# A fused gather, gated FFN and residual on one NeuronCore: the per-tile quantisation of the hidden layer rebuilt

## The chip, the cores and the metric

One NeuronCore of a Trainium2 chip runs the whole program. The metric is the device time of one execution in microseconds (us); lower is better. The engines are PE (TensorE), DVE (VectorE), ACT (ScalarE), POOL (GpSimd) and SP (SyncE, which here only starts DMAs). Each works through its own instruction stream in order, and streams meet only at semaphores.

## The reference

The input is 1024 rows (32 batches of 32 channels) by 256 features. Cut to what matters:

```python
w  = cond_weights[itok]                                   # one 32x32 matrix per batch
xc = einsum('bct,bcd->bdt', x, w)                         # small mix of channels
def act_quant(x):                                         # row-wise, 8 bits
    scale = 127.0 / clip(max|x|, 1e-4)
    return clip(round(x * scale), -128, 127) / scale
def linear_bit(x, w, g):                                  # w ternary: round(tanh(w/mean|w|)) * arctanh(mean|w|)
    return einsum('bsd,od->bso', act_quant(g * x * rsqrt(mean(x*x) + 1e-8)), ternary(w))
h   = silu(linear_bit(xc, w1, g1)) * linear_bit(xc, w2, g2)   # 256 -> 1024
out = x + linear_bit(h, w3, g3)                               # 1024 -> 256
```

The part of interest is the last line's quantisation of h: for each row, the mean of the squares of 1024 hidden values, the largest |h * g3|, the rounding of h * g3 to integers of at most 127, and a factor that puts the scale back after the last matmul.

## The kernel before

Rows are cut into 8 tiles of 128 (TILES). A head loads and ternarises the three weight matrices, gathers the small matrices, mixes the channels and quantises x; it lasts until about 34 us. Then a pipeline over the tiles runs. Its stages for tile t, each a closure of that name on one engine:

- PE `up_a(t)`, `up_v(t)`: four 128x512 matmuls each into a_ps and v_ps. Both accumulators exist once, so `up_a(t+1)` waits for `silu(t)` and `up_v(t+1)` for `hidden(t)`.
- ACT `silu(t)` (L399) reads a_ps and writes gate. DVE `hidden(t)` (L551) multiplies v_ps, its scale and gate into hid.
- POOL L325 writes hg = hid * g3 for the whole 1024 columns. ACT `squares(t)` (L406) sums hid squared into h_ss and throws the squares away.
- POOL `h_roots(t)`: two [128,1] steps (L309, L311) and a power (L316) on two columns give the root of the mean square and its inverse.
- DVE `peak_of(t)` (L560) is an absolute maximum over hg, `step_of` (L566) and `scale_of` (L574) turn it into the step and its reciprocal.
- ACT `rounding(t)` (L413) writes hr = hg * scale + a large constant, in fp32; the integer, plus 1536, then stands as an fp16 number in the low half of each word.
- PE `h_turn(t)` (L758) transposes these halves into t_ps, DVE `keep_h(t)` (L581) subtracts 1536 and writes bf16, PE `down(t)` (L769) multiplies with the third weight, POOL `h_deq_of(t)` (L302) forms the output factor, DVE `residual(t)` (L588) adds the result to x_sb, and SP stores the tile.

Buffers of hid, hg, hr and of the statistics are two deep. The order on each engine is written out by hand. POOL does, for t = 0 to 6: L325 of t, `h_roots(t)`, `h_deq_of(t-1)`. For the last tile POOL does no L325: DVE does that product itself (`gain_last`, L596) and also the rounding (`rounding_last`, L602). At the end PE runs `h_turn(7)`, `down(6)`, `down(7)`.

Two operations of the head matter below: POOL's `round_w` (L237, one operation over 2048 columns) and DVE's `diagonal` (L446, four small copies from SBUF to SBUF).

Of the kernel before, what the change touches and what calls it, by code (L numbers as in the profile page):

```python
# [6 lines left out]
FP16 = mybir.dt.float16  # L7
INT32 = mybir.dt.int32
# [5 lines left out]
P = 128  # L14
# [14 lines left out]

OFFSET = 1536.0  # L30
# [3 lines left out]
def adaln_ffn(nc, x, cond, cond_w, w1, g1, w2, g2, w3, g3, out):  # L34
    ctx = ExitStack()
    with ctx:
# [44 lines left out]
        h_sq_junk = sb("h_sq_junk", [P, 2, HID], BF16)  # L81
# [13 lines left out]
        hid = sb("hid", [P, 2, HID])  # L95
        hg = sb("hg", [P, 2, HID])
        hr = sb("hr", [P, 2, HID])
        hq_t = sb("hq_t", [P, 2, KH, P], BF16)
        h_ss = sb("h_ss", [P, 2])
        h_base = sb("h_base", [P, 2, 2])  # L100
        h_root = sb("h_root", [P, 2, 2])
        h_peak = sb("h_peak", [P, 2])
        h_step = sb("h_step", [P, 2])
        h_scale = sb("h_scale", [P, 2])
        h_deq0 = sb("h_deq0", [P, 2])
# [34 lines left out]
        xr_last, hr_last = sem("xr_last"), sem("hr_last")  # L140
        hg_last = sem("hg_last")
        hss_ready, hg_ready, hbase_ready, hroot_ready = sem("hss_ready"), sem("hg_ready"), sem("hbase_ready"), sem("hroot_ready")
        hpeak_ready, hstep_ready, hscale_ready, hdeq0_ready = sem("hpeak_ready"), sem("hstep_ready"), sem("hscale_ready"), sem("hdeq0_ready")
        hr_ready, ht_ready, hq_ready, y_ready, out_ready = sem("hr_ready"), sem("ht_ready"), sem("hq_ready"), sem("y_ready"), sem("out_ready")
# [49 lines left out]
        def _(pool):  # L194
# [18 lines left out]
            pool.memset(minus_one[:], -1.0).then_inc(roots_made, 1)  # L213
            pool.memset(cw_diag[:], 0.0).then_inc(diag_zero, 1)
# [66 lines left out]
            pool.wait_ge(roots_made, 3)  # L281
# [49 lines left out]
            h_deq_of(TILES - 1)

        @block.scalar
        def _(act):
# [56 lines left out]
            logarithm()  # L391
            act.wait_ge(xdeq_ready, 2)
# [22 lines left out]

            silu(0)
            for t in range(TILES):
                if t + 1 < TILES:
                    silu(t + 1)
                squares(t)  # L420
                if t >= 1:
                    rounding(t - 1)

        @block.vector
        def _(dve):
# [118 lines left out]
            def hidden(t):  # L544

                dve.wait_ge(gate_ready, t + 1)
                dve.wait_ge(v_ready, t + 1)
                if t >= 2:
                    dve.wait_ge(hss_ready, t - 1)
                    dve.wait_ge(hg_ready, t - 1)  # L550
                dve.scalar_tensor_tensor(hid[:, t % 2], v_ps[:], x_deq[:, 1, t // 2, t % 2:t % 2 + 1], gate[:, t % 2],  # L551
                                         ALU.mult, ALU.mult).then_inc(hid_ready, 1)

            def peak_of(t):
                b = slice(t % 2, t % 2 + 1)
                if t < TILES - 1:
                    dve.wait_ge(hg_ready, t + 1)
                else:
                    dve.wait_ge(hg_last, 1)
                dve.tensor_reduce(h_peak[:, b], hg[:, t % 2], AX.X, ALU.max, apply_absolute_value=True).then_inc(hpeak_ready, 1)  # L560

            def step_of(t):
                b = slice(t % 2, t % 2 + 1)
                dve.wait_ge(hpeak_ready, t + 1)
                dve.wait_ge(hroot_ready, t + 1)
                dve.tensor_scalar(h_step[:, b], h_peak[:, b], 1.0 / QMAX, h_root[:, t % 2, 0:1],  # L566
                                  ALU.mult, ALU.max).then_inc(hstep_ready, 1)

            def scale_of(t):
                b = slice(t % 2, t % 2 + 1)  # L570
                dve.wait_ge(hstep_ready, t + 1)
                if t >= 2:
                    dve.wait_ge(hr_ready, t - 1)
                dve.reciprocal(h_scale[:, b], h_step[:, b]).then_inc(hscale_ready, 1)  # L574

            def keep_h(t):

                dve.wait_ge(ht_ready, t + 1)
                if t >= 2:
                    dve.wait_ge(y_ready, t - 1)  # L580
                dve.tensor_scalar(hq_t[:, t % 2], t_ps[t % 2][:, :].rearrange("p (j n) -> p j n", j=KH), -OFFSET, None,  # L581
                                  ALU.add).then_inc(hq_ready, 1)

            def residual(t):

                dve.wait_ge(y_ready, t + 1)
                dve.wait_ge(hdeq0_ready, t + 1)
                dve.scalar_tensor_tensor(x_sb[:, t], y_ps[t % 2][:, 0:FEAT], h_deq0[:, t % 2:t % 2 + 1], x_sb[:, t],  # L588
                                         ALU.mult, ALU.add).then_inc(out_ready, 1)

            def gain_last(t):

                dve.wait_ge(hid_ready, t + 1)
                dve.wait_ge(hr_ready, t - 1)
                dve.wait_ge(g3_in, 16)
                dve.tensor_tensor(hg[:, t % 2], hid[:, t % 2], g3_all[:], ALU.mult).then_inc(hg_last, 1)  # L596

            def rounding_last(t):

                dve.wait_ge(hscale_ready, t + 1)  # L600
                dve.wait_ge(ht_ready, t - 1)
                dve.tensor_scalar(hr[:, t % 2], hg[:, t % 2], h_scale[:, t % 2:t % 2 + 1], ROUNDER,  # L602
                                  ALU.mult, ALU.add).then_inc(hr_last, 1)

            hidden(0)
            x_keep(3)
            hidden(1)
            peak_of(0)
            step_of(0)
            keep_w(2, 0)  # L610
            scale_of(0)
            keep_w(2, 1)
            for t in range(2, TILES - 1):
                hidden(t)
                peak_of(t - 1)
                if t >= 3:
                    residual(t - 3)
                step_of(t - 1)
                keep_h(t - 2)
                scale_of(t - 1)  # L620

            last = TILES - 1
            hidden(last)
            peak_of(last - 1)
            gain_last(last)
            step_of(last - 1)
            residual(last - 3)
            scale_of(last - 1)
            keep_h(last - 2)
            peak_of(last)  # L630
            step_of(last)
# [181 lines left out]
```

## Time and profile before

| | us |
|---|---|
| median of 3 runs | 77.32 |
| lowest and highest | 76.74, 77.88 |
| span of the profiled execution (first to last instruction) | 76.6 |
| busy: PE, DVE, ACT, POOL | 48.0, 58.1, 47.7, 55.4 |

The profiled execution's own time is not among those listed; the three runs lie 0.1 to 1.3 above its span. Busy sums cover head and pipeline together, so what the pipeline is limited by has to be read from the time lines of its engines. In those, each line gives start, duration, engine, source line, operation and output<-inputs; in brackets stands idle time before it and what ended it. Two consecutive operations of an engine can overlap by up to 0.1 us, so the distance of two starts is a little shorter than the duration.

### The profile page before, as it was taken

How to read it: one execution, taken by the hardware profiler on the slowest of the kernel's cores; microseconds unless marked ns; L12 is line 12 of the kernel's file. 1: busy time of each engine (PE TensorE's matmuls, PEld its weight loads, DVE VectorE, ACT ScalarE, POOL GpSimd, SP SyncE). 2: the span in 40 equal slices, each digit the busy share in tenths (PEclk: the TensorE clock that was granted, in tenths of full speed). 3: DMA queues.
4: the chain of work that ended last, by engine and by line, in shares of the span. 5: the costliest groups of instructions: out<-in, count | busy, mean ns of one | idle time of the engine just before them, and what ended most of it. 6: DMA issues, size and time to landing. Idle time of an engine off the chain costs nothing.

```text
span 76.6 us, 1068 instructions
## 1 busy us (share of the span) xinstructions
PE 48.0 (63%) x298; PEld 31.3 (41%) x302; DVE 58.1 (76%) x117; ACT 47.7 (62%) x70; POOL 55.4 (72%) x97
## 2 busy tenths in 40 slices
PE   0200509995829803999897298977888471079960
PEld 0200408774526702355461155544545250078730
DVE  0203278989999999967699989979797979996340
ACT  5014508599909995995859959896979783410000
POOL 6788777264938977989689898999999999810100
PEclk9999999999975895556999999999999999855589
DMA  0599989963710000000000000010202020010222
GB/s 0 119 385 346 327 237 278 330 210 115 253 71 0 0 0 4 0 9 4 0 0 0 0 0 4 17 52 9 68 0 68 0 68 0 23 45 0 68 68 68
DMA packets 5369, 6.22 MB, mean 81 GB/s; under 512 B 500, under 2 KB 4980, under 8 KB 5364
## 3 DMA queue, kind: packets, MB, share of 16 engines
q1 hardware_dynamic: 5108, 6.03, 24.6%
q0 software_dynamic: 256, 0.13, 0.8%
q8 instruction: 2, 0.03, 0.2%
q14 instruction: 3, 0.02, 0.1%
HBM read 5.11 MB, written 1.05 MB: 80 GB/s over the span
## 4 chain that ended last, share of the span: by engine, by line
DVE 24%; issue 22%; POOL 22%; DMA 12%; PE 11%; ACT 4%; SPq 0%; POOLq 0%; DVEq 0%
DMA w_sb<-in_L_ffn_w 12%; POOL hg L325 11%; PE y_ps L769 6%; DVE xg L477 6%; DVE cw_diag L446 5%; DVE x_peak L482 5%; PE a_ps L652 3%; PE t_ps L758 2%; POOL h_deq L302 2%; DVE hid L551 2%; ACT hr L413 2%; DVE abs_sum L438 2%; POOL h_root L316 2%; POOL h_base L311 2%; POOL h_base L309 1%
## 5 line engine op out<-in xcount | busy, mean ns | idle before, releaser
L325 POOL TENSOR_TENSOR hg<-hid,g_all 128x1024 f32<-128x1024 f32 x7 | 16.5, 2358 | 0.8 <-DVE hid L551 0.8
L413 ACT ACTIVATE hr<-hg,rounder,h_scale 128x1024 f32<-128x1024 f32 x7 | 8.7, 1241 | 5.5 <-DVE h_scale L574 5.5
L769 PE MATMUL y_ps<-w_t,hq_t 128*128 128x256 bf16 x64 | 10.3, 319 | 2.1 <-DVE hq_t L581 2.0
L560 DVE TENSOR_REDUCE h_peak<-hg 128x1 f32<-128x1024 f32 x8 | 9.7, 1217 | 1.7 <-POOL hg L325 1.6
L551 DVE SCALAR_TENSOR_TENSOR hid<-v_ps,x_deq,gate 128x1024 f32<-128x1024 f32 x8 | 10.2, 1271 | 0.9 <-PE v_ps L725 0.6
L725 PE MATMUL v_ps<-w_t,xq_t 128*128 128x512 bf16 x30 | 8.9, 415 | 3.0 <-DVE hid L551 2.9
L399 ACT ACTIVATE gate<-a_ps,x_deq 128x1024 f32<-128x1024 f32 x8 | 8.8, 1100 | 2.2 <-PE a_ps L725 2.1
L725 PE MATMUL a_ps<-w_t,xq_t 128*128 128x512 bf16 x30 | 8.7, 407 | 1.8 <-issue 1.3
L218 POOL DMA_INDIRECT cw_rows<-in_L_cond_weights,row_idx x8 | 7.9, 982 | 2.4 <-issue 2.1
L769 PEld LDWEIGHTS y_ps<-w_t,hq_t 128*128 128x128 bf16 x64 | 6.9, 115 | 5.6 <-DVE hq_t L581 4.1
L652 PE MATMUL a_ps<-x_sb,cw_diag 128*128 128x256 f32 x16 | 7.0, 597 | 2.5 <-DVE cw_diag L446 2.5
L758 PE MATMUL t_ps<-ident,hr 128*128 128x128 f16 x64 | 5.8, 243 | 4.2 <-ACT hr L413 4.2
L406 ACT ACTIVATE h_sq_junk<-hid 128x1024 bf16<-128x1024 f32 x8 | 8.4, 1046 | 0.0
L341 ACT ACTIVATE abs_values<-w_sb 128x1024 bf16<-128x1024 f32 x4 | 4.2, 1061 | 5.2 <-DMA w_sb<-in_L_ffn_w 5.2
L346 ACT ACTIVATE w_sb<-w_sb,inv_mean 128x2048 f32<-128x2048 f32 x3 | 6.0, 1999 | 2.2 <-DVE inv_mean L455 2.2
L667 PE MATMUL y_ps<-abs_sum,ones 128*128 128x1 f32 x12 | 2.5, 317 | 7.6 <-DVE abs_sum L438 7.2
L758 PEld LDWEIGHTS t_ps<-ident,hr 128*128 128x128 f16 x64 | 4.8, 110 | 6.0 <-ACT hr L413 4.7
L438 DVE TENSOR_REDUCE abs_sum<-w_sb 128x1 f32<-128x1024 f32 x2 | 2.4, 1220 | 5.4 <-DMA w_sb<-in_L_ffn_w 5.4
L302 POOL TENSOR_SCALAR h_deq<-h_step,h_root,atanh 128x1 f32<-128x1 f32 x8 | 3.6, 455 | 3.5 <-DVE x_sb L588 3.5
L316 POOL TENSOR_TENSOR h_root<-h_base,roots 128x2 f32<-128x2 f32 x8 | 5.6, 702 | 0.7
L725 PEld LDWEIGHTS v_ps<-w_t,xq_t 128*128 128x128 bf16 x32 | 2.8, 104 | 7.8 <-DVE hid L551 5.0
L581 DVE TENSOR_SCALAR hq_t<-t_ps 128x1024 bf16<-128x1024 f16 x8 | 5.5, 683 | 0.6 <-PE t_ps L758 0.6
(76 smaller groups left out, 99.9 us busy)
## 6 DMA issues: line engine op xcount, KB each, us to landing
w_sb<-in_L_ffn_w SPq DMA_DIRECT2D x6, 512.0 KB, 4.5
x_sb<-in_x SPq DMA_DIRECT2D x4, 256.0 KB, 3.1
out<-x_sb SPq DMA_DIRECT2D x8, 128.0 KB, 1.7
g_all<-in_L_ffn_g SPq DMA_DIRECT2D x1, 512.0 KB, 4.3
g<-in_L_ffn_g SPq DMA_DIRECT2D x2, 128.0 KB
cw_rows<-in_L_cond_weights,row_idx POOLq DMA_INDIRECT x8, 4.3
cond_i<-in_itok_B SPq DMA_DIRECT2D x1, 0.1 KB
```

What stands on the lines that cost most here:

```text
L218: pool.indirect_dma_start(cw_rows[:, t, :], None, cond_rows, bass.IndirectOffsetOnAxis(ap=row_idx[:, t:t + 1].bitcast(UINT32), axis=0)).th ...
L316: pool.tensor_tensor(h_root[:, b], h_base[:, b], roots[:, :, 0], ALU.pow).then_inc(hroot_ready, 1)
L325: pool.tensor_tensor(hg[:, b], hid[:, b], g3_all[:], ALU.mult).then_inc(hg_ready, 1)
L399: act.activation(gate[:, t % 2], a_ps[:], ACT.Silu, scale=x_deq[:, 0, t // 2, t % 2:t % 2 + 1]).then_inc(gate_ready, 1)
L406: act.activation(h_sq_junk[:, t % 2], hid[:, t % 2], ACT.Square, accum_out=h_ss[:, t % 2:t % 2 + 1]).then_inc(hss_ready, 1)
L413: act.activation(hr[:, t % 2], hg[:, t % 2], ACT.Identity, scale=h_scale[:, t % 2:t % 2 + 1], bias=rounder[:]).then_inc(hr_ready, 1)
L551: dve.scalar_tensor_tensor(hid[:, t % 2], v_ps[:], x_deq[:, 1, t // 2, t % 2:t % 2 + 1], gate[:, t % 2], ALU.mult, ALU.mult).then_inc(hid_ ...
L560: dve.tensor_reduce(h_peak[:, b], hg[:, t % 2], AX.X, ALU.max, apply_absolute_value=True).then_inc(hpeak_ready, 1)
L652: last = pe.matmul(xc_ps[p % 2][:, i, :], cw_diag[:, 2 * p + i, :], x_sb[:, 2 * p + i, :], start=True, stop=True)
L725: last = pe.matmul(ps[:, n * HALF:(n + 1) * HALF], xq_t[:, which, c, t * P:(t + 1) * P], w_t[which][:, c, n * HALF:(n + 1) * HALF], start= ...
L758: last = pe.transpose(t_ps[t % 2][:, j * P:(j + 1) * P], low_half(hr[:, t % 2, j * P:(j + 1) * P]), ident[:])
L769: last = pe.matmul(y_ps[t % 2][:, 0:FEAT], hq_t[:, t % 2, j, :], w_t[2][:, j, :], start=(j == 0), stop=(j == KH - 1))
```

## The change

- POOL's product with g3 covers only columns 0 to 511 (SPLIT).
- ACT's `squares` keeps its squares, in fp32, in h_sq. Once before the pipeline ACT also squares g3/127 into g3_sq. The peak is then the maximum of h_sq * g3_sq, one `tensor_tensor_reduce` on DVE.
- Step, its inverse and the root are all taken with one POOL power over three columns, after one [128,1] step (`base`) and one [128,2] step that takes the maximum with the peak.
- The rounding is the conversion to int16 on write: POOL (`rounding_p`) multiplies its half of hg, DVE (`rounding_v`) computes hid * factor * g3 for columns 512 to 1023 in one operation. No constant is added, and no 1536 has to be taken off.
- The eviction of t_ps (`keep_h`) goes from DVE to ACT, which no longer rounds; for the last tile it stays on DVE.
- POOL handles all 8 tiles alike; `gain_last` and `rounding_last` are gone. hid is three deep, the statistics four.
- PE runs `down(t-2)` after `up_v(t+1)` and `h_turn(t-1)`.

```diff
+            def gain(t):
                 pool.wait_ge(hid_ready, t + 1)
                 if t >= 2:
+                    pool.wait_ge(hr_p, t - 1)
+                pool.tensor_tensor(hg[:, t % 2], hid[:, t % DEPTH, 0:SPLIT], g3_all[:, 0:SPLIT], ALU.mult).then_inc(hg_ready, 1)
+            def base(t):
+                pool.wait_ge(hss_ready, t + 1)
...
+                pool.tensor_scalar(h_base[:, r, 2:3], h_ss[:, r:r + 1], 1.0 / HID, EPS, ALU.mult, ALU.add).then_inc(hbase_ready, 1)
+            def roots_of(t):
+                pool.wait_ge(hbase_ready, t + 1)
+                pool.wait_ge(hpeak_ready, t + 1)
+                pool.tensor_scalar(h_base[:, r, 0:2], h_base[:, r, 2:3].to_broadcast([P, 2]), FLOOR_STEP ** 2, h_peak[:, r:r + 1],
+                                   ALU.mult, ALU.max).then_inc(hstep_ready, 1)
...
+                pool.tensor_tensor(h_root[:, r], h_base[:, r], h_roots[:], ALU.pow).then_inc(hroot_ready, 1)
+            def rounding_p(t):
+                pool.wait_ge(hroot_ready, t + 1)
...
+                pool.tensor_scalar(hr[:, t % 2, 0:SPLIT], hg[:, t % 2], h_root[:, t % RING, 0:1], 1.0, ALU.mult, ALU.mult).then_inc(hr_p, 1)
+            def deq_of(t):
...
+                pool.tensor_scalar(h_deq[:, r:r + 1], h_root[:, r, 1:2], h_root[:, r, 2:3], atanh[:, 2:3],
+                                  ALU.mult, ALU.mult).then_inc(hdeq_ready, 1)
+            for t in range(TILES):
+                gain(t)
+                base(t)
+                roots_of(t)
+                rounding_p(t)
+                deq_of(t)
...
             logarithm()
+            act.wait_ge(g3_in, 16)
+            act.activation(g3_sq[:], g3_all[:], ACT.Square, scale=1.0 / QMAX).then_inc(g3sq_ready, 1)
             act.wait_ge(xdeq_ready, 2)
...
             silu(0)
             for t in range(TILES):
+                squares(t)
                 if t + 1 < TILES:
                     silu(t + 1)
-                squares(t)
                 if t >= 1:
-                    rounding(t - 1)
+                    keep_h(t - 1)
...
+            def peak_of(t):
+                dve.wait_ge(hss_ready, t + 1)
...
+                dve.tensor_tensor_reduce(hg_sq[:], h_sq[:, t % 2], g3_sq[:], 1.0, 0.0, ALU.mult, ALU.max,
+                                         h_peak[:, r:r + 1]).then_inc(hpeak_ready, 1)
+            def rounding_v(t):
+                dve.wait_ge(hroot_ready, t + 1)
...
+                dve.scalar_tensor_tensor(hr[:, t % 2, SPLIT:], hid[:, t % DEPTH, SPLIT:], h_root[:, t % RING, 0:1], g3_all[:, SPLIT:],
+                                         ALU.mult, ALU.mult).then_inc(hr_v, 1)
             hidden(0)
             x_keep(3)
+            peak_of(0)
             hidden(1)
             keep_w(2, 0)
             keep_w(2, 1)
+            rounding_v(0)
+            for t in range(1, TILES):
+                peak_of(t)
+                if t + 1 < TILES:
+                    hidden(t + 1)
+                if t >= 3:
+                    residual(t - 3)
+                rounding_v(t)
```

## Rows read from the trace of the kernel before

**Rows 1.** The page, the chain that ended last: shares of the span.
```profile
DVE 24%; issue 22%; POOL 22%; DMA 12%; PE 11%; ACT 4%; SPq 0%; POOLq 0%; DVEq 0%
```
**Rows 2.** Time line of ACT where the pipeline starts.
```profile
33.09 1.28 ACT L372 ACT_TABLE_LOAD   x1
34.47 1.11 ACT L399 ACTIVATE gate<-a_ps,x_deq 128x1024 f32<-128x1024 f32 x1
```
**Rows 3.** Time line of POOL, one turn of the pipeline; start us, us, operation.
```profile
52.76 2.35 POOL L325 TENSOR_TENSOR hg<-hid,g_all 128x1024 f32<-128x1024 f32 x1
55.19 0.19 POOL L309 TENSOR_SCALAR h_base<-h_ss 128x1 f32<-128x1 f32 x1
...
55.73 0.70 POOL L316 TENSOR_TENSOR h_root<-h_base,roots 128x2 f32<-128x2 f32 x1
56.44 0.34 POOL L302 TENSOR_SCALAR h_deq<-h_step,h_root,atanh 128x1 f32<-128x1 f32 x1
56.74 2.36 POOL L325 TENSOR_TENSOR hg<-hid,g_all 128x1024 f32<-128x1024 f32 x1
```
**Rows 4.** Busy time by stretch: PE, PEld, DVE, ACT, POOL, granted clock, DMA.
```profile
48.80:52.80 4.00, 3.53 (x27) 1.94 (x25) 3.59 (x7) 3.64 (x6) 3.75 (x7) 1.00 0.10 33
...
64.50:68.00 3.50, 0.60 (x6) 0.61 (x7) 3.46 (x7) 1.24 (x1) 2.62 (x5) 0.78 0.11 37
```
**Rows 5.** The chain that ended last, in order of time: its end.
```profile
70.14 0.85 PE t_ps L758 x8
...
73.97 0.48 DVE x_sb L588
```
**Rows 6.** Groups by line and form; columns: busy us, mean ns | idle before, releaser.
```profile
L325 POOL TENSOR_TENSOR hg<-hid,g_all 128x1024 f32<-128x1024 f32 x7 | 16.5, 2358 | 0.8 <-DVE hid L551 0.8
...
L551 DVE SCALAR_TENSOR_TENSOR hid<-v_ps,x_deq,gate 128x1024 f32<-128x1024 f32 x8 | 10.2, 1271 | 0.9 <-PE v_ps L725 0.6 <-ACT gate L399 0.3
L560 DVE TENSOR_REDUCE h_peak<-hg 128x1 f32<-128x1024 f32 x8 | 9.7, 1217 | 1.7 <-POOL hg L325 1.6
...
L399 ACT ACTIVATE gate<-a_ps,x_deq 128x1024 f32<-128x1024 f32 x8 | 8.8, 1100 | 2.2 <-PE a_ps L725 2.1
...
L406 ACT ACTIVATE h_sq_junk<-hid 128x1024 bf16<-128x1024 f32 x8 | 8.4, 1046 | 0.0
...
L588 DVE SCALAR_TENSOR_TENSOR x_sb<-y_ps,h_deq,x_sb 128x256 f32<-128x256 f32 x8 | 3.8, 478 | 2.3 <-PE y_ps L769 2.3
L237 POOL TENSOR_SCALAR w_sb<-w_sb 128x2048 f32<-128x2048 f32 x2 | 3.8, 1904 | 0.0
...
L243 POOL TENSOR_SCALAR xr<-xg,x_scale 128x256 f32<-128x256 f32 x6 | 2.8, 477 | 1.6 <-DVE x_scale L493 1.5
...
L365 ACT ACTIVATE w_t<-t_ps,neg_offset 128x1024 bf16<-128x1024 f16 x2 | 2.2, 1098 | 0.0
```
**Rows 7.** Time line of POOL in the head: a long operation and two powers.
```profile
19.88 1.91 POOL L237 TENSOR_SCALAR w_sb<-w_sb 128x2048 f32<-128x2048 f32 x1
...
25.82 0.86 POOL L261 TENSOR_TENSOR lg<-lg,minus_one 128x3 f32<-128x3 f32 x1
...
32.00 0.98 POOL L269 TENSOR_TENSOR lg<-lg,minus_one 128x3 f32<-128x3 f32 x1
```
**Rows 8.** Time line of DVE in the head, the small copies.
```profile
11.69 0.90 DVE L446 COPY cw_diag<-cw_rows 32x64 f32<-32x64 f32 x4
...
20.15 2.33 DVE L446 COPY cw_diag<-cw_rows 32x64 f32<-32x64 f32 x4
```
**Rows 9.** Time line of DVE and POOL together, tiles 6 and 7.
```profile
64.26 1.22 DVE L596 TENSOR_TENSOR hg<-hid,g_all 128x1024 f32<-128x1024 f32 x1
64.43 1.26 POOL L302 TENSOR_SCALAR h_deq<-h_step,h_root,atanh 128x1 f32<-128x1 f32 x1
```
**Rows 10.** Time line of DVE at the end of the head.
```profile
32.06 1.14 DVE L502 TENSOR_SCALAR xr<-xg,x_scale 128x256 f32<-128x256 f32 x4
```

More of the change, by code:

```diff
@@ L7 @@
 FP16 = mybir.dt.float16
+INT16 = mybir.dt.int16
 INT32 = mybir.dt.int32
@@ L27 @@
 FLOOR_STEP = FLOOR / QMAX
+SPLIT = 512
+DEPTH = 3
+RING = 4
 OFFSET = 1536.0
@@ L94, in adaln_ffn @@
         gate = sb("gate", [P, 2, HID])
-        hid = sb("hid", [P, 2, HID])
-        hg = sb("hg", [P, 2, HID])
-        hr = sb("hr", [P, 2, HID])
-        hq_t = sb("hq_t", [P, 2, KH, P], BF16)
[L99 to L105, printed above, removed]
+        hid = sb("hid", [P, DEPTH, HID])
+        h_sq = sb("h_sq", [P, 2, HID])
+        g3_sq = sb("g3_sq", [P, HID])
+        hg_sq = sb("hg_sq", [P, HID], BF16)
+        hg = sb("hg", [P, 2, SPLIT])
+        hr = sb("hr", [P, 2, HID], INT16)
+        hq_t = sb("hq_t", [P, 2, KH, P], BF16)
+        h_ss = sb("h_ss", [P, RING])
+        h_peak = sb("h_peak", [P, RING])
+        h_base = sb("h_base", [P, RING, 3])
+        h_root = sb("h_root", [P, RING, 3])
+        h_roots = sb("h_roots", [P, 3])
+        h_deq = sb("h_deq", [P, RING])
         a_ps = ctx.enter_context(nc.psum_tensor("a_ps", [P, HID], FP32))
@@ L547, in hidden @@
                 dve.wait_ge(v_ready, t + 1)
[L548 to L551, printed above, removed]
+                if t >= DEPTH:
+                    dve.wait_ge(hss_ready, t - DEPTH + 1)
+                    dve.wait_ge(hg_ready, t - DEPTH + 1)
+                dve.scalar_tensor_tensor(hid[:, t % DEPTH], v_ps[:], x_deq[:, 1, t // 2, t % 2:t % 2 + 1], gate[:, t % 2],
@@ L578, in keep_h, with keep_h_last @@
+            def keep_h_last(t):
                 dve.wait_ge(ht_ready, t + 1)
[L579 to L582, printed above, removed]
+                dve.wait_ge(y_ready, t - 1)
+                dve.tensor_copy(hq_t[:, t % 2], t_ps[t % 2][:, :].bitcast(INT16).rearrange("p (j n) -> p j n", j=KH)).then_inc(hq_last, 1)
@@ L584, in residual @@
             def residual(t):
+                r = t % RING
                 dve.wait_ge(y_ready, t + 1)
-                dve.wait_ge(hdeq0_ready, t + 1)
-                dve.scalar_tensor_tensor(x_sb[:, t], y_ps[t % 2][:, 0:FEAT], h_deq0[:, t % 2:t % 2 + 1], x_sb[:, t],
+                dve.wait_ge(hdeq_ready, t + 1)
+                dve.scalar_tensor_tensor(x_sb[:, t], y_ps[t % 2][:, 0:FEAT], h_deq[:, r:r + 1], x_sb[:, t],
                                          ALU.mult, ALU.add).then_inc(out_ready, 1)
[L591 to L596, printed above, removed]
@@ L629, in _ @@
-            keep_h(last - 2)
-            peak_of(last)
-            step_of(last)
-            scale_of(last)
-            rounding_last(last)
-            keep_h(last - 1)
-            residual(last - 2)
-            keep_h(last)
-            residual(last - 1)
-            residual(last)
+                rounding_v(t)
+            residual(TILES - 3)
+            keep_h_last(TILES - 1)
+            residual(TILES - 2)
+            residual(TILES - 1)
         @block.tensor
@@ L757, in h_turn @@
                 for j in range(KH):
-                    last = pe.transpose(t_ps[t % 2][:, j * P:(j + 1) * P], low_half(hr[:, t % 2, j * P:(j + 1) * P]), ident[:])
+                    last = pe.transpose(t_ps[t % 2][:, j * P:(j + 1) * P], hr[:, t % 2, j * P:(j + 1) * P].bitcast(FP16), ident[:])
                 last.then_inc(ht_ready, 1)
             def down(t):
-                pe.wait_ge(hq_ready, t + 1)
+                if t < TILES - 1:
+                    pe.wait_ge(hq_ready, t + 1)
+                else:
+                    pe.wait_ge(hq_last, 1)
                 if t >= 2:
@@ L778, in _ @@
                     up_a(t + 1)
-                if t >= 3:
-                    down(t - 3)
-                if t + 1 < TILES:
                     up_v(t + 1)
@@ L785, in _ @@
                     w_turn(2, 1)
+                if t >= 1:
+                    h_turn(t - 1)
                 if t >= 2:
-                    h_turn(t - 2)
-            h_turn(TILES - 2)
-            down(TILES - 3)
+                    down(t - 2)
             h_turn(TILES - 1)
```

129 lines of the change are left out of this document (42 added, 87 removed).

## The prediction

> **What bounds the kernel now.** I read the chain of waits first: no engine has more than a quarter of it [rows 1], so the stages have to be taken apart. The head ends when ACT starts the first `silu` at 34.47 [rows 2]. Behind it the time line of POOL is closed: between two starts of L325 lie 56.74 - 52.76 = 3.98 us, filled without a gap by the product (2.36), two small steps, the power (0.70) and `h_deq` (0.34) [rows 3]. The other engines have slack in such a turn: of 4.00 us PE is busy 3.53, DVE 3.59, ACT 3.64, and POOL's 3.75 are its durations without the gaps of 0.08 between dependent steps [rows 4]. So POOL sets the pace of the pipeline, about 4.0 us per tile. The drain is the last transposes, two `down` and the last residual [rows 5].
>
> **POOL's own work per tile.** Removed: half of the product. Between 2358 ns for 1024 columns and about 190 ns for one of one column, half the columns cost 190 + 1084 = 1.27 us [rows 3, 6]. Two small steps (0.27 from start to start each) stay two. The power has three columns instead of two: 0.86 and 0.98 for a 128x3 power [rows 7] against 0.70; I take 0.98. Added is `rounding_p`, 512 columns from one tensor: from 477 ns at 256 and 1904 at 2048 columns [rows 6], 0.797 ns a column, 0.68 us. That it writes int16 is shown by no row; bounds: 0.68 and, at the rate of the two-input product, 1.27. I take 0.68, since reading one tensor is what it shares with those rows. `deq` stays (0.34, 0.30 to the next start). From start to start: 1.35 + 0.27 + 0.27 + 1.05 + 0.68 + 0.30 = 3.92. POOL, the bound, is thus not relieved: 3.98 becomes 3.92.
>
> **The other engines.** DVE loses the reduction (1.22), step, reciprocal (0.4) and eviction (0.68), and gains the multiply-and-max and `rounding_v`. The former is on no row; the nearest are the 1024-column operations of 1217 and 1271 ns [rows 6], the upper bound is two passes, 2.4. I take 1.22. `rounding_v`: 1271 at 1024 and 478 at 256 columns give 1.035 ns a column, 0.74 us for 512. Its turn is 1.22 + 1.27 + 0.48 + 0.74 = 3.7, less overlaps 3.4. ACT: 1.10 + 1.24 + 1.10 = 3.4; the fp32 squares are costed as the bf16 ones, the eviction at L365's 1.10 with 1.0 as the other end [rows 6]. PE does the same work. All of this is under POOL's turn and costs nothing there; if POOL's turn were under 3.4 they would be next. The deeper rings only take away waits, and none of these is in POOL's closed turn. The two added memsets and their wait stand before the gathers on POOL; DVE's first copy out of the gathered rows starts at 11.69 without having waited for them [rows 8]. I take nothing; some 0.3 us is the most, if that cover were gone.
>
> **What the change adds to the path: the port that DVE and POOL share.** Two places of the trace show the two engines excluding each other. At 64.43 POOL's `h_deq` of one column takes 1.26 instead of 0.34; everything it waits for by semaphore is past by then, but DVE's L596, a product of two tensors in SBUF, runs 64.26 to 65.48, and `h_deq` ends at 65.69, 0.21 behind it [rows 3, 9]. The other way round, DVE's four copies take 2.33 instead of 0.90, while POOL's L237 runs 19.88 to 21.79 [rows 7, 8]. And the pipeline of before avoids the clash: its `hidden` has one SBUF tensor (v_ps is in PSUM), its reduction one, its evictions none, and L325 takes 2.36 beside them each time. The changed DVE operations do not: the multiply-and-max reads h_sq and g3_sq, `rounding_v` reads hid and g3_all, all in SBUF, in each tile. A power is an exception: L269 (32.00, 0.98) runs beside DVE's four L502, which take 1.14 for all four, so neither waited for the other's end [rows 7, 10], 0.12 above the other power at most.
>
> Now the circle of dependences from power(t) to power(t+1). On POOL: `rounding_p`, `deq`, `gain`, `base`, step, power. On DVE behind power(t): `rounding_v(t)`, then `peak_of(t+1)`, for which POOL's step of t+1 waits. `hidden` and `residual` (no clash) fall under the power. The two clashing DVE operations thus lie where POOL has only reading work to do. Waiting hides the start of the blocked operation, so a blocked one costs its columns: by DVE's 0.96 to 1.03 ns a column 0.56 for `rounding_v`, 1.10 for the peak; of POOL's small one behind DVE 0.21 [rows 9]. Sum: 0.07 + 0.66 `rounding_p` + 0.56 + 0.21 `deq` + 0.05 + 1.25 `gain` + 1.10 peak + 0.15 `base` + 0.27 step + 0.98 power = 5.30; with the peak before `gain`, where nothing hides `gain`'s start, 5.48. I take 5.4 per tile.
>
> That DVE's two-input operation also waits while POOL is reading is not on these rows: the copy in [rows 8] is of another kind. If only POOL waits, the peak overlaps what POOL has begun: 5.1. I take 5.4, both ways, since each engine has been seen waiting for the other once. The Trainium skill, page "SBUF — State Buffer", section "Who interferes with whom", has it go both ways: a DVE instruction with two SBUF inputs contends with a GpSimd instruction that reads SBUF, and whichever starts first keeps the pair for the whole instruction. By that rule the turn is the 5.4, without it 5.1; the trace agrees with the half of it that has POOL waiting (1.26 for 0.34).
>
> **The start.** ACT's square of g3 (1.05 by L406 [rows 6]) comes behind the table load, which ends at 34.37, and in front of `silu(0)`, which nothing else holds back by more than 0.1 [rows 2]: `silu(0)` moves to 35.4. Nothing is there to cover it, 0.95. `hidden(0)` follows 0.1 behind its end, 36.6 to 37.85, `squares(0)`, now first in ACT's queue, to 39.1, `gain(0)` to 39.25, the peak 39.25 to 40.4, `base`, step and power to 42.0. (`silu(1)`, queued behind `squares(0)`, ends at 40.2, in time for `hidden(1)` at 40.4.) Without the clash power(0) ends at 41.75.
>
> **The end.** Power(7) ends at 42.0 + 7 x 5.4 = 79.8. Both halves of the rounding, one after the other: 0.07 + 0.66 + 0.56, hr is there at 81.1, PE starts at 81.2. From `h_turn(7)` on the order is the old one, and from its start at 70.14 to the end of the span were 6.46 us [rows 5]: 87.7. PE had fallen to a lower clock there (0.78 in the stretch before [rows 4]) after waiting, and will have waited again. The span is 76.6 and the median 77.32, so 0.7 is added: 88.4, rounded to **88.5**, 14% above before.
>
> **Rivals.**
> A, the likeliest, is this: exclusion, 5.1 to 5.5 per tile. With the first operation not waiting, 7 x 0.3 less: 86.3; with `rounding_p` at 1.27, 4.7 more: 93.1.
> B, no exclusion for these forms, against which the one case of [rows 9] speaks (it is a single one, and behind a [128,1] operation; no row has a long POOL operation against DVE's two-tensor read): POOL's 3.92 is the turn; 41.75 + 27.4 + 0.1 + 0.74 + 0.1 + 6.46 = 76.6, plus 0.7: 77.3, no change. It is the case on the other side, and decides if the two clashing operations together cost under 0.2 per tile (8 x 0.2 = 1.6, 2%). Below 75.8 it would have to be that also power and gain are at their lower ends, 0.86 and half of 2.36 (0.2 a tile, 1.6 in all): 75.7.
> C, the exclusion is shared by columns, not by whole instructions, so that half of the 1.5 us remains: 4.65 per tile; 42.0 + 32.6 + 1.4 + 6.46 + 0.7 = 83.1. The 1.26 of [rows 9] speaks against it, since a one-column operation would have slipped in.
> D, multiply-and-max takes two passes, 2.4: 1.1 a tile more than A, 97. Nothing in the trace speaks for it; no row of such an operation exists.
> E, the clock falls inside the pipeline, since PE then works 3.5 of 5.4 instead of 3.5 of 4.0. At the lower level PE's own work would be near the turn; it stayed at 1.00 in all full turns before [rows 4]. It would add one to three us to A.
>
> **How the numbers follow.** A 0.70, E (with A) 0.05, C 0.08, B 0.10, D 0.07. Slower by over 2%: all of A, E, C and D less the 0.01 that the upper end of C's sharing could leave unmeasurable: 0.89. Within 2%: B but for 0.03, and that 0.01: 0.08. Faster: the lower ends of B, 0.03. (2% is about what a measurement of this kernel tells from no change.) The range is that of A with its bounds and of C at its low end: 82.5 to 93.5. It leaves out B and D and the edge of C, 2 in 10.
>
> **What would show it.** Right: `gain` and `rounding_p` on POOL with some instances far above 1.27 and 0.68, or the small POOL steps at over 1 us, just when DVE's multiply-and-max or `rounding_v` runs; a POOL turn of 5.1 to 5.5; the first `silu` about 0.95 later, behind the square of g3. Wrong: turns near 3.9 with POOL's durations at their bare values (B), DVE's peak at 2.4 (D), granted clock under 1.00 in the middle (E). The forecast falls if the clashing operations find POOL idle or in its power more often than the circle above allows.

## The result and the profile after

The changed kernel takes 90.51 us (median of 4 runs, 88.83 to 91.15) against 77.6 for the one before. Some executions of most kernels here are in a slower state, and leaving those out (two of the four of the changed kernel, the profiled one among them) it takes 1.157 times as long, 95% interval 1.137 to 1.178. By the medians it is slower by 12.9 us, inside the predicted range of 82.5 to 93.5 and 2.0 above the 88.5.

| us | before | after |
|---|---|---|
| span of the profiled execution | 76.6 | 89.4 |
| busy PE, DVE, ACT, POOL | 48.0, 58.1, 47.7, 55.4 | 51.0, 55.9, 47.5, 68.3 |
| POOL's turn in the pipeline | 3.98 | 5.57 |

The profiled execution of the changed kernel is its longest one, 91.15; the other three have spans of 88.4, 87.1 and 89.1. DVE and ACT have less to do than before, PE the same operations, and POOL, which gave up half of the product and got half of the rounding, should have the same work by the prediction's count (3.92 for 3.98 a tile); yet it is busy for 13 us more. That contradiction is the case. In what follows a turn is the distance between two starts of the same operation in consecutive tiles, and a bare duration is the one that an operation has when nothing holds it. The first place to look is the time line of POOL, one turn (start us, us, operation; it answers [rows 3]):

```profile
53.10 2.30 POOL L337 TENSOR_SCALAR hr<-hg,h_root 128x512 int16<-128x512 f32 x1
55.38 0.34 POOL L344 TENSOR_SCALAR h_deq<-h_root,atanh 128x1 f32<-128x1 f32 x1
55.68 1.27 POOL L308 TENSOR_TENSOR hg<-hid,g_all 128x512 f32<-128x512 f32 x1
57.03 0.19 POOL L316 TENSOR_SCALAR h_base<-h_ss 128x1 f32<-128x1 f32 x1
57.33 0.29 POOL L323 TENSOR_SCALAR h_base<-h_base,h_peak 128x2 f32<-128x2 f32 x1
57.70 0.87 POOL L329 TENSOR_TENSOR h_root<-h_base,h_roots 128x3 f32<-128x3 f32 x1
58.67 2.30 POOL L337 TENSOR_SCALAR hr<-hg,h_root 128x512 int16<-128x512 f32 x1
```

From start to start: 2.28 + 0.30 + 1.35 + 0.30 + 0.37 + 0.97 = 5.57, and the six full turns from 47.52 to 80.98 are all 5.57 or 5.58. Every operation has its expected length (the power 0.87 where 0.98 was taken) but `rounding_p` (L337), 2.30 for work of 0.69. Its bare length is in this trace too: for tile 0 it takes 0.70, at 42.04, while DVE evicts w_t from PSUM. Now DVE in the same stretch:

```profile
53.03 0.75 DVE L596 SCALAR_TENSOR_TENSOR hr<-hid,h_root,g_all 128x512 int16<-128x512 f32 x1 [2.49 <-POOL h_root L329]
53.70 1.22 DVE L588 CUSTOM_DVE_ANT_0 hg_sq<-h_sq,g_sq 128x1024 bf16<-128x1024 f32 x1
54.84 0.08 DVE L588 DVE_READ_ACCUMULATOR2_ANT h_peak<- 128x1 f32 x1
54.89 1.28 DVE L578 SCALAR_TENSOR_TENSOR hid<-v_ps,x_deq,gate 128x1024 f32<-128x1024 f32 x1
```

`rounding_v` and the multiply-and-max (the custom operation L588, with its accumulator read) run 53.03 to 54.92, and `rounding_p`, started 0.07 later, ends 0.48 behind them. It is the picture of [rows 9], now in the six tiles 1 to 6 and behind two DVE operations in a row. A third view, the groups by line (busy us, mean ns | idle before), shows what waits for what elsewhere:

```profile
L337 POOL TENSOR_SCALAR hr<-hg,h_root 128x512 int16<-128x512 f32 x8 | 15.7, 1966 | 0.8
L596 DVE SCALAR_TENSOR_TENSOR hr<-hid,h_root,g_all 128x512 int16<-128x512 f32 x8 | 6.0, 750 | 15.6 <-POOL h_root L329 15.6
...
L440 ACT ACTIVATE hq_t<-t_ps 128x1024 bf16<-128x1024 int16 x7 | 7.2, 1024 | 14.6 <-PE t_ps L748 14.6
```

DVE stands 15.6 us in front of `rounding_v` until POOL's power is done, ACT 14.6 in front of the eviction: POOL's closed turn is what all others wait for. POOL never stands idle in these turns, so its busy share reads as work what is in part waiting inside an operation.

Between the two profiled executions 12.8 us divide like this. Power(0) ends at 41.94, before at 40.82 (+1.1). From there to the end of power(7) pass 38.94, before 26.19 (+12.75; of this 7 x 1.59 = 11.1 are the turn of 5.57 against 3.98, the rest mostly that the last turn used to be 2.59, the last tile's product being done by DVE). From power(7) to the end pass 8.5, before 9.6 (-1.1).

### The profile page after: what moved, and what is told of

It reads as the page before. It is cut to its first block, busy times and chain, and to the rows that moved or that the text cites. A ratio compares the mean times of both kernels' runs of the same rounds, so it can differ in the third digit from the quotient of the medians.

```text
span 89.4 us, 1071 instructions
## 1 busy us (share of the span) xinstructions
PE 51.0 (57%) x298; PEld 31.9 (36%) x302; DVE 55.9 (62%) x108; ACT 47.5 (53%) x71; POOL 68.3 (76%) x108
## 3 DMA queue, kind: packets, MB, share of 16 engines
HBM read 5.11 MB, written 1.05 MB: 69 GB/s over the span
## 4 chain that ended last, share of the span: by engine, by line
POOL 32%; DVE 22%; PE 13%; issue 11%; DMA 10%; ACT 7%; POOLq 2%; SPq 0%; DVEq 0%
DMA w_sb<-in_L_ffn_w 10%; POOL hg L308 10%; POOL hr L337 8%; POOL h_root L329 7%; PE y_ps L762 6%; DVE xg L504 5%; DVE cw_diag L473 4%; DVE x_peak L509 4%; POOL h_deq L344 3%; POOL h_base L316 2%; PE a_ps L644 2%; POOL h_base L323 2%; PE t_ps L748 2%; DVE hg_sq L588 2%; POOLq L40 1%
## 5 line engine op out<-in xcount | busy, mean ns | idle before, releaser
L337 POOL TENSOR_SCALAR hr<-hg,h_root 128x512 int16<-128x512 f32 x8 | 15.7, 1966 | 0.8
L596 DVE SCALAR_TENSOR_TENSOR hr<-hid,h_root,g_all 128x512 int16<-128x512 f32 x8 | 6.0, 750 | 15.6 <-POOL h_root L329 15.6
L440 ACT ACTIVATE hq_t<-t_ps 128x1024 bf16<-128x1024 int16 x7 | 7.2, 1024 | 14.6 <-PE t_ps L748 14.6
L308 POOL TENSOR_TENSOR hg<-hid,g_all 128x512 f32<-128x512 f32 x8 | 11.1, 1387 | 1.7 <-DVE hid L578 1.7
L762 PE MATMUL y_ps<-w_t,hq_t 128*128 128x256 bf16 x64 | 12.2, 360 | 0.0
L717 PE MATMUL a_ps<-w_t,xq_t 128*128 128x512 bf16 x28 | 10.2, 481 | 3.5 <-ACT gate L423 1.9
L578 DVE SCALAR_TENSOR_TENSOR hid<-v_ps,x_deq,gate 128x1024 f32<-128x1024 f32 x8 | 10.2, 1281 | 1.7 <-ACT gate L423 1.7
L717 PE MATMUL v_ps<-w_t,xq_t 128*128 128x512 bf16 x32 | 10.1, 447 | 0.8 <-DVE hid L578 0.8
L432 ACT ACTIVATE h_sq<-hid 128x1024 f32<-128x1024 f32 x8 | 8.4, 1051 | 3.6 <-DVE hid L578 3.6
L588 DVE CUSTOM_DVE_ANT_0 hg_sq<-h_sq,g_sq 128x1024 bf16<-128x1024 f32 x8 | 9.8, 1226 | 0.6 <-ACT h_sq L432 0.6
L329 POOL TENSOR_TENSOR h_root<-h_base,h_roots 128x3 f32<-128x3 f32 x8 | 7.0, 870 | 0.7
```

Source lines behind the costliest of these rows:

```text
L308: pool.tensor_tensor(hg[:, t % 2], hid[:, t % DEPTH, 0:SPLIT], g3_all[:, 0:SPLIT], ALU.mult).then_inc(hg_ready, 1)
L329: pool.tensor_tensor(h_root[:, r], h_base[:, r], h_roots[:], ALU.pow).then_inc(hroot_ready, 1)
L337: pool.tensor_scalar(hr[:, t % 2, 0:SPLIT], hg[:, t % 2], h_root[:, t % RING, 0:1], 1.0, ALU.mult, ALU.mult).then_inc(hr_p, 1)
L432: act.activation(h_sq[:, t % 2], hid[:, t % DEPTH], ACT.Square, accum_out=h_ss[:, t % RING:t % RING + 1]).then_inc(hss_ready, 1)
L578: dve.scalar_tensor_tensor(hid[:, t % DEPTH], v_ps[:], x_deq[:, 1, t // 2, t % 2:t % 2 + 1], gate[:, t % 2], ALU.mult, ALU.mult).then_inc( ...
L588: dve.tensor_tensor_reduce(hg_sq[:], h_sq[:, t % 2], g3_sq[:], 1.0, 0.0, ALU.mult, ALU.max, h_peak[:, r:r + 1]).then_inc(hpeak_ready, 1)
```

## Experiments

The first four runs test the suspected clash: two take one of the two clashing operations away, the third both, and the fourth puts one into the kernel before. The rival is that the wait is not at a port but in the circle of dependences. The kernels of these four compute other values than the reference, since each leaves out or changes a factor; the amount of work is what their times are about. The diffs are shortened (semaphore calls, and indices as [...]).

**The peak from one tensor.**
```diff
-dve.tensor_tensor_reduce(hg_sq[:], h_sq[:, t % 2], g3_sq[:], 1.0, 0.0, ALU.mult, ALU.max, h_peak[:, r:r + 1])
+dve.tensor_reduce(h_peak[:, r:r + 1], h_sq[:, t % 2], AX.X, ALU.max)
```


> The changed kernel with the peak as a plain maximum over h_sq (one tensor in SBUF; the factor g3 squared is left out of the peak). Same length on DVE, 1.22 us. Theory (the port of DVE's second SBUF tensor and of POOL excludes): rounding_p and what follows is no longer held for the 1.14 us of the peak, POOL's turn falls from 5.57 to about 4.4, total 90.5 - 8 x 1.14 = 81.4. Rival (the circle of dependences alone makes the turn long; rounding_p at 2.3 is merely a record that includes waiting for a semaphore): the peak still stands in the circle with the same length, 90.5.

Measured: 83.08 us (81.80 to 83.37), 1.062 times before (1.046 to 1.078), 7.4 less than the changed kernel, where 9.1 were expected. The reduction is as long as the operation it replaces, 1.21 for 1.22, and stands at the same place of the circle. It reads one tensor, and it also no longer writes a product of 1024 columns; the next run tells these two apart. In its time line, POOL and DVE together:

```profile
59.97 0.75 DVE L595 SCALAR_TENSOR_TENSOR hr<-hid,h_root,g_all 128x512 int16<-128x512 f32 x1 [1.06 <-POOL h_root L329]
60.04 1.25 POOL L337 TENSOR_SCALAR hr<-hg,h_root 128x512 int16<-128x512 f32 x1
60.64 1.21 DVE L588 TENSOR_REDUCE h_peak<-h_sq 128x1 f32<-128x1024 f32 x1
...
64.57 1.25 POOL L337 TENSOR_SCALAR hr<-hg,h_root 128x512 int16<-128x512 f32 x1
```

`rounding_p` now ends 0.57 behind `rounding_v` and runs on beside the reduction. The turn is 4.53 where 4.4 was expected, 0.09 of it because `rounding_p` ends 0.57 behind the operation it waited for and not 0.48. The total fell by less than expected, because the expectation multiplied by 8 and there are seven turns: 7 x 1.04 = 7.3. The rival, which expected no change, falls.

**The rounding from one tensor.**
```diff
-dve.scalar_tensor_tensor(hr[:, t % 2, SPLIT:], hid[:, t % DEPTH, SPLIT:], h_root[...], g3_all[:, SPLIT:], ALU.mult, ALU.mult)
+dve.tensor_scalar(hr[:, t % 2, SPLIT:], hid[:, t % DEPTH, SPLIT:], h_root[...], 0.0, ALU.mult, ALU.add, accum_out=hr_sum[:])
```


> The changed kernel with rounding_v reading hid alone (a tensor times scalar with an accumulator, so that it reads at one element a cycle; the factor g3 is left out on columns 512 to 1023). Theory: rounding_p starts beside it and is held only once the peak begins; the 0.67 of rounding_v goes from the turn, 5.57 to 4.9, total about 85. If rounding_p can slip in before the peak altogether, the peak then has to wait for it instead, with the same sum. Rival (dependences alone): 90.5.

Measured: 85.63 us (84.12 to 86.14), 1.108 (1.097 to 1.119), for about 85 expected. In its time line, POOL and DVE together:

```profile
61.50 0.69 POOL L338 TENSOR_SCALAR hr<-hg,h_root 128x512 int16<-128x512 f32 x1
...
62.10 1.22 DVE L589 CUSTOM_DVE_ANT_0 hg_sq<-h_sq,g_sq 128x1024 bf16<-128x1024 f32 x1
62.16 1.37 POOL L345 TENSOR_SCALAR h_deq<-h_root,atanh 128x1 f32<-128x1 f32 x1
...
63.49 1.27 POOL L309 TENSOR_TENSOR hg<-hid,g_all 128x512 f32<-128x512 f32 x1
```

`rounding_p` has its bare 0.69 beside the 0.75 of DVE, and the wait has moved to the next POOL operation that finds the multiply-and-max (62.10 to 63.32) running: `deq`, 1.37 instead of 0.34. The turn is 5.0. DVE's operation still writes the same 512 columns of hr, and takes as long, so what held POOL is its second SBUF input and not its output. `hidden` says the same of the old form: a `scalar_tensor_tensor` with one input in PSUM, 54.89 to 56.17 in the changed kernel, it leaves `gain` beside it (55.68) its bare 1.27.

**Both.**

> The changed kernel with both edits of the two runs before: no DVE operation of the pipeline reads two SBUF tensors. Theory: POOL's turn is the sum of its own bare durations, 0.70 + 0.30 + 1.35 + 0.28 + 0.38 + 0.97 = 3.98, total 90.5 - 8 x 1.6 = 77.7, the time of the kernel before. Rival: 90.5.

Measured: 78.95 us (78.45 to 79.30), 1.017 (1.006 to 1.027). The turn, from its time line of POOL:

```profile
58.04 0.69 POOL L338 TENSOR_SCALAR hr<-hg,h_root 128x512 int16<-128x512 f32 x1
...
62.02 0.69 POOL L338 TENSOR_SCALAR hr<-hg,h_root 128x512 int16<-128x512 f32 x1
```

3.98 us, the sum of POOL's bare durations. So the prediction's 3.92 for POOL without the clash was near, and the clash is worth 5.57 - 3.98 = 1.59 per turn and 11.6 us of the whole; the two edits alone took 1.04 and 0.57, so they add up. The total is 1.25 above the 77.7 expected, which had taken off eight times 1.6 where there are seven turns (90.5 - 11.1 = 79.4). Without the clash the rebuilt work would still not be faster than before.

**The clash put into the kernel before.**
```diff
-dve.tensor_reduce(h_peak[:, b], hg[:, t % 2], AX.X, ALU.max, apply_absolute_value=True)
+dve.tensor_tensor_reduce(hg_junk[:], hg[:, t % 2], hg[:, t % 2], 1.0, 0.0, ALU.mult, ALU.max, h_peak[:, b])
```


> The kernel before with one edit: its peak is a multiply-and-max of hg with itself, two SBUF inputs, in place of the reduction (the square root is left out, so the scale differs). Theory: POOL's small steps and its next product are held for the peak's 1.14 in each of 7 or 8 tiles, POOL's turn goes from 3.98 to about 5.1, total 77.6 + 8 to 9 = 86. Rival (no exclusion, the changed kernel is slow for its dependences): 77.6.

Measured: 85.28 us (84.49 to 85.38), 1.097 (1.085 to 1.109), 7.4 more than the 77.86 of the kernel before beside it. In its time line, POOL and DVE together:

```profile
59.28 1.23 DVE L561 CUSTOM_DVE_ANT_0 hg_junk<-hg 128x1024 bf16<-128x1024 f32 x1 [0.52 <-POOL hg L326]
59.33 1.23 POOL L310 TENSOR_SCALAR h_base<-h_ss 128x1 f32<-128x1 f32 x1
...
60.64 0.19 POOL L312 TENSOR_SCALAR h_base<-h_ss 128x1 f32<-128x1 f32 x1
```

A [128,1] step that takes 0.19 in [rows 3] takes 1.23 when a two-input operation of DVE runs, even though both inputs are the same tensor, and the turn is 5.02 for the 5.1 expected. One edit of DVE's peak, none of what POOL does, and the kernel before has more than half of the slowdown.

The same run shows where the wait ends, in its last tile, where DVE has two such operations one after the other, with the accumulator read of the first between them:

```profile
69.33 1.22 DVE L561 CUSTOM_DVE_ANT_0 hg_junk<-hg 128x1024 bf16<-128x1024 f32 x1 [0.52 <-POOL hg L326]
69.38 1.22 POOL L310 TENSOR_SCALAR h_base<-h_ss 128x1 f32<-128x1 f32 x1
...
70.48 1.22 DVE L598 TENSOR_TENSOR hg<-hid,g_all 128x1024 f32<-128x1024 f32 x1
70.68 1.07 POOL L312 TENSOR_SCALAR h_base<-h_ss 128x1 f32<-128x1 f32 x1
```

POOL's step gets in between them: it ends at 70.60, though the second product runs from 70.48 to 71.70, and only the next step is held. In the changed kernel `rounding_v` and the multiply-and-max follow each other with nothing between, and there POOL is held through both.

**Who waits when POOL is first.** In all turns shown above DVE starts first, so they say nothing on the direction that the prediction left open. A [128,1] reciprocal between power and `rounding_v` turns the order round.

```diff
 dve.wait_ge(hroot_ready, t + 1)
+dve.reciprocal(late[:], ones[:, 0:1]).then_inc(late_done, 1)
+dve.wait_ge(late_done, t + 1)
```


> The changed kernel with one [128,1] operation of DVE between the power and rounding_v, so that POOL's rounding_p starts first. If DVE's two-tensor operation waits for a POOL operation that runs: rounding_p takes its bare 0.69, rounding_v is recorded with about 1.2 instead of 0.75, deq waits for the peak; the turn is 0.1 + 0.69 + 1.75 + 0.2 + 1.35 + 0.28 + 0.38 + 0.97 = 5.7, total 91. If only POOL waits: both roundings run side by side, the turn is about 5.25, total 88.

Measured: 89.85 us (89.35 to 90.17), 1.166 (1.160 to 1.173). In its time line, POOL and DVE together:

```profile
58.16 0.69 POOL L339 TENSOR_SCALAR hr<-hg,h_root 128x512 int16<-128x512 f32 x1
58.29 1.10 DVE L600 SCALAR_TENSOR_TENSOR hr<-hid,h_root,g_all 128x512 int16<-128x512 f32 x1
58.83 1.82 POOL L346 TENSOR_SCALAR h_deq<-h_root,atanh 128x1 f32<-128x1 f32 x1
59.31 1.21 DVE L590 CUSTOM_DVE_ANT_0 hg_sq<-h_sq,g_sq 128x1024 bf16<-128x1024 f32 x1
```

`rounding_p` has its bare length, `rounding_v` is recorded with 1.10 for 0.75 and ends at 59.39, 0.54 behind POOL's 58.85: the 512 columns alone, its start hidden in the wait. DVE waits too, and so the rule of the Trainium skill that the prediction cites ("SBUF — State Buffer", section "Who interferes with whom") holds in both directions here. `deq`, next on POOL, then waits for both DVE operations, 1.82 for 0.34. The opening says that streams meet only at semaphores; these two engines also meet at the port that they share. The turn is 5.46, neither the 5.7 nor the 5.25 expected: the 5.7 had counted in full what waiting hides. It is near the 5.48 of the prediction, which had this order but for `deq`: there `deq` came before the peak, here it comes behind it.

**The square of g3.**
```diff
             keep_w_a(1)
+            act.wait_ge(g3_in, 16)
+            act.activation(g3_sq[:], g3_all[:], ACT.Square, scale=1.0 / QMAX).then_inc(g3sq_ready, 1)
             x_round(2)
             logarithm()
```


> The changed kernel with ACT's square of g3 moved from behind the table load to between keep_w_a(1) and x_round(2), where ACT stood idle for 0.86 us. By the term of the sum (0.95 on the path at the start): the first silu starts about 0.9 earlier, the total is 90.5 - 0.9 = 89.6. If something else holds the start back, 90.5.

Measured: 89.75 us (88.36 to 89.96). The time line of ACT has `silu(0)`, first in the changed kernel and then in this one:

```profile
34.51 1.06 ACT L415 ACTIVATE g_sq<-g_all 128x1024 f32<-128x1024 f32 x1
35.48 1.10 ACT L423 ACTIVATE gate<-a_ps,x_deq 128x1024 f32<-128x1024 f32 x1
```
```profile
29.62 1.05 ACT L413 ACTIVATE g_sq<-g_all 128x1024 f32<-128x1024 f32 x1
...
34.59 1.11 ACT L423 ACTIVATE gate<-a_ps,x_deq 128x1024 f32<-128x1024 f32 x1
```

The start moves by 0.89, as the term said. The difference of the medians, 0.8, is of that size but within the scatter of the runs; the trace carries the claim, not the totals. From `rounding_p` to `rounding_p` this execution has 63.39 - 57.81 = 5.58, as the changed kernel.

**No share for POOL.** SPLIT is 0, `gain` and `rounding_p` are gone and DVE rounds all 1024 columns.

> The changed kernel without POOL's half of the product and of the rounding: SPLIT is 0, DVE does all 1024 columns in rounding_v. By the exclusion: POOL has only small steps and the power left, which wait at most for the end of a DVE operation, so DVE sets the turn with 1.14 + 1.20 + 0.39 + 1.19 = 3.9, at most 4.1 with the small steps that wait; total 78 to 79.5. By the view that DVE's longer work in the circle is the bound (dependences alone), the turn would be the 5.57 plus 0.5 for the longer rounding_v less nothing: 94.

Measured: 79.89 us (79.72 to 81.72), 1.036 (1.030 to 1.041); 10.6 less than the changed kernel, though DVE has 0.5 us a tile more to do. In its time line of POOL:

```profile
59.30 2.48 POOL L343 TENSOR_SCALAR h_deq<-h_root,atanh 128x1 f32<-128x1 f32 x1
...
63.51 2.48 POOL L343 TENSOR_SCALAR h_deq<-h_root,atanh 128x1 f32<-128x1 f32 x1
```

A product of one column takes 2.48: it ends at 61.78, 0.13 behind both operations of DVE (59.23 to 61.65). The turn is 4.21 where 3.9 to 4.1 was expected, the total 0.4 above the expectation: `deq`, two steps and the power come behind the peak and DVE waits 0.19 for them in each turn. The view that the dependences alone make the turn long, which expected 94, falls once more. Dividing elementwise work between the two engines had made it slower than giving all of it to one.

**A version that beats both.** If POOL sets the turn of the kernel before and nothing clashes in its full turns, the way to be faster is to take a step off POOL:
```diff
-act.activation(h_sq_junk[:, t % 2], hid[:, t % 2], ACT.Square,
+act.activation(h_sq_junk[:, t % 2], hid[:, t % 2], ACT.Square, scale=FLOOR_STEP / HID ** 0.5,
...
-pool.tensor_scalar(h_base[:, b, 0:1], h_ss[:, b:b + 1], FLOOR_STEP ** 2 / HID, FLOOR_STEP ** 2 * EPS, ALU.mult, ALU.add)
-pool.tensor_scalar(h_base[:, b, 1:2], h_ss[:, b:b + 1], 1.0 / HID, EPS, ALU.mult, ALU.add)
+pool.tensor_scalar(h_base[:, b:b + 1], h_ss[:, b:b + 1], 1.0, FLOOR_STEP ** 2 * EPS, ALU.mult, ALU.add)
-pool.tensor_tensor(h_root[:, b], h_base[:, b], roots[:, :, 0], ALU.pow)
+pool.tensor_tensor(h_root[:, b], h_base[:, b:b + 1].to_broadcast([P, 2]), roots[:, :, 0], ALU.pow)
```


> The kernel before with one small POOL step less per tile: ACT's squares are scaled so that one [128,1] step gives the argument of both powers, which read it twice; one [128,1] product more, once, ahead of the pipeline. POOL sets the turn of the kernel before: 3.98 - 0.27 = 3.71, over 8 tiles 2.1 us less, 77.6 - 2.1 = 75.5. If the power on a repeated input costs 0.1 more, 76.3. If DVE (3.5 per turn) or PE (3.5) can't follow, between.

Measured: 75.8 us (75.43 to 76.93, 6 runs), 0.984 times before (0.978 to 0.990), for 75.5 expected. Its turn on POOL is 59.40 - 55.67 = 3.73:

```profile
55.67 2.36 POOL L326 TENSOR_TENSOR hg<-hid,g_all 128x1024 f32<-128x1024 f32 x1
58.11 0.19 POOL L312 TENSOR_SCALAR h_base<-h_ss 128x1 f32<-128x1 f32 x1
58.39 0.70 POOL L317 TENSOR_TENSOR h_root<-h_base,roots 128x2 f32<-128x2 f32 x1
59.10 0.34 POOL L305 TENSOR_SCALAR h_deq<-h_step,h_root,atanh_f 128x1 f32<-128x1 f32 x1
59.40 2.35 POOL L326 TENSOR_TENSOR hg<-hid,g_all 128x1024 f32<-128x1024 f32 x1
```

The turn is 0.25 shorter, and PE's transposes of tile 6 start at 66.06 where they started at 67.39. The profiled spans, 74.1 and 76.6, differ by more than these 1.33: from there to the last residual passed 5.39 for 6.58, the eight transposes alone taking 0.62 for 1.03 at another granted clock (0.74 in the stretch of 66 to 68 us, for 0.62). That part is not shown to come from the edit.

**One more step off POOL.** On top of that, `h_deq` moves to DVE.

> The kernel of the run before_one_base, and in addition the small product for the output factor (h_deq) goes from POOL to DVE, behind the eviction. POOL's turn 3.72 - 0.30 = 3.42; DVE's rises from 3.6 by 0.1 and becomes the bound at 3.65 to 3.7: 0.2 to 0.5 us less in all, 75.4 against 75.8. If the small product reads SBUF in a way that clashes with POOL's long product (its operands are [128,1]; no such clash is on record), DVE would wait up to 2.3 per tile and the time goes above 85.

Measured: 77.0 us (76.25 to 77.61), 0.988 (0.982 to 0.995) of the kernel before measured beside it. Against the 0.984 (0.978 to 0.990) of the version it builds on this is no gain that can be told, and the expected 0.2 to 0.5 did not come. POOL is relieved and now waits 0.29 in each turn; DVE has no gap left, the moved product being recorded with 0.27, and the turn is 3.70. The busy time by stretch (PE, PEld, DVE, ACT, POOL, clock) says it in one line, DVE 4.00 of 4.00:

```profile
52.00:56.00 4.00, 3.61 (x31) 2.15 (x30) 4.00 (x9) 3.58 (x6) 3.54 (x4) 1.00 0.12 37
```

A turn shorter by 0.03 would be 0.2 in all, less than the runs scatter. That the median lies 1.2 above that of the version before has two parts on record. The time stands 1.9 to 2.05 above the span in these executions, 1.7 to 1.8 in all the others; why is open. And of the 1.2 between the two profiled spans 1.0 is the drain, from the transposes of tile 6 to the last residual: 66.35 to 72.70, for 66.06 to 71.45. PE came out of its wait at a granted clock of 0.50 in the stretch of 66 to 68 us, for 0.74, and its eight transposes took 1.03 for 0.62. Whether the edit has a part in that is not shown.

## Why the prediction was right, point by point

- **What bounds, and that POOL is not relieved.** Right, with 0.06 to spare: 3.92 predicted without the clash, 3.98 in the run with both one-tensor edits.
- **The clash.** Right, both its existence for these two operations and that they fall where POOL has only reading work. Its worth was put at 5.4 - 3.92 = 1.5 per tile, measured 5.57 - 3.98 = 1.59. Two of its premises need a word. By its own 0.96 to 1.03 ns a column (the 0.96 follows from no row) the blocked operations would cost 0.49 to 0.53 and 0.98 to 1.06, not 0.56 and 1.10; the 0.54 of the run in which DVE is second lies between. And [rows 7, 10] do not show a power to be an exception, since L502 reads one SBUF tensor, and POOL's plain product L270, which starts at 33.05 beside its end, has its bare 0.20 as well. The run with the clash in the kernel before does show one, in its last tile, for a power that starts first: both have their bare lengths.

```profile
73.50 0.70 POOL L317 TENSOR_TENSOR h_root<-h_base,roots 128x2 f32<-128x2 f32 x1
...
73.82 1.22 DVE L561 CUSTOM_DVE_ANT_0 hg_junk<-hg 128x1024 bf16<-128x1024 f32 x1
```

- **The order within the turn.** The sum had POOL's `rounding_p` first. In fact DVE is first, by 0.07, and its two operations follow each other without letting POOL in: `rounding_p` is recorded with 2.30. POOL first gives 5.46 (the run in which DVE is second), the real order 5.57. Against the sum of 5.30, from the start of `rounding_p` to the end of `gain` passed 3.93 for 3.83, by another order and so in part by luck; `base` and the step took 0.67 for 0.42, since `base` was thought to hide in a wait and does not; the power took 0.97 for 1.05. The 5.4, taken between 5.30 and 5.48, was too short by 0.17, or 1.2 us in seven.
- **Prices of unknown operations.** Multiply-and-max 1.22 (1.22 taken; the two passes of rival D don't exist), the conversion to int16 on POOL 0.69 (0.68 taken), `rounding_v` 0.75 (0.74), half the product 1.26 (1.27), eviction on ACT 1.02 (1.10 taken, 1.0 the other end).
- **The start.** 35.48 for `silu(0)` where 35.4 was said; power(0) ended at 41.94 for 42.0. The run with the early square shows that the 0.95 was on the path (0.89). The times between were off in both directions: `base(0)`, held by the peak, took 1.04.
- **The end.** From the start of `h_turn(7)` 7.12 instead of 6.46. The last stretches of the chain, first before, then here:

```profile
70.14 0.85 PE t_ps L758 x8
70.99 2.96 PE y_ps L769 x16
```
```profile
82.28 1.04 PE t_ps L748 x8
83.32 3.43 PE y_ps L762 x16
```

  That is 0.19 and 0.47 more. PE's granted clock was 0.50 to the end here; before it had risen to a mean of 0.67 in the stretch of 72 to 74 us.
- **From span to time.** The 0.7 was mis-sized. The profiled execution of 76.6 is not the one of the median: in the runs whose spans are listed the time is 1.7 above the span for both kernels (78.03 against 76.3; 90.14 against 88.4). The predicted span of 87.7 lies between the 87.1 and 88.4 of two executions; with 1.7 instead of 0.7 it would have been 89.4 us. So the 88.4 is 2.8 below the profiled execution's 91.15 (1.1 to power(7), 0.7 in the end, 1.0 here), all to one side, and 2.0 below the median.
- **Rivals.** B (no exclusion) falls with the runs that take the clash out or put it in. D falls, the multiply-and-max taking 1.22. C (sharing by columns) falls: a one-column `deq` takes 2.48. E: the clock did fall inside the pipeline of the profiled execution, by the busy time by stretch,

```profile
48.00:54.00 6.00, 4.13 (x22) 2.37 (x23) 3.51 (x6) 2.37 (x5) 5.62 (x7) 0.72 0.00 1
54.00:60.00 6.00, 3.94 (x27) 2.09 (x26) 3.96 (x6) 3.92 (x5) 5.62 (x7) 1.00 0.06 22
60.00:66.00 6.00, 4.76 (x24) 2.84 (x24) 3.91 (x7) 3.10 (x4) 5.62 (x7) 0.72 0.08 25
```

  to a mean of 0.72 in two stretches, each after PE had waited over 2 us for hr (2.92 and 2.36). A third wait, of 2.36 up to 72.19, was not followed by a fall (1.00 from 72 to 74 us), so the length of the wait does not settle it. The turns stayed at 5.57 and 5.58 throughout: PE has slack there. The fall was among the rivals, but its price of one to three us was wrong: in the turns it was none.

## What to carry to other kernels

Before work is divided between VectorE and GpSimd, count for each VectorE operation how many of its inputs lie in SBUF. With two, GpSimd's reading work next to it was held in every run here, save the power, and so the division can cost more than it saves: 1.59 us a tile, with nothing saved on GpSimd's own work. An engine that a profile shows as busy all the time may be waiting inside its operations; the sign is one operation whose length is far from others of its shape. And a short step taken off the engine that sets the turn (0.25 a tile) gained 1.6% in all, where a rebuild of the whole turn cost 16%.

## What was not expected of the hardware

- GpSimd waits not for one VectorE operation but for the whole run of two that follow each other: 2.30 for `rounding_p`, 2.48 for a one-column product, when nothing stands between them. Behind the second comes an accumulator read of 0.08, and `hidden` with its one SBUF input lets GpSimd through. Where such a read stood between two products with two inputs each, GpSimd's step got in (70.60, above); that the read makes the gap is likely by this one case, not tested.
- Waiting hides the fixed part of an operation, which the prediction assumed, and in both directions: 512 columns on VectorE end 0.54 behind the one they waited for, 0.75 when alone; 512 on GpSimd end 0.48 or 0.57 behind, 0.69 when alone.
- A VectorE product with a scalar that also writes an accumulator (0.75 for 512 columns) left GpSimd its bare 0.69, as a plain reduction does.
- The two inputs need not be different: hg times hg made GpSimd's [128,1] step take 1.23 for 0.19.
